# A three-phase audio tower: the last phase's five instruction streams in another order, routing cut in two

## The reference

```
tok:   pad the 750 rows to 3 segments of 256, take every second row -> 3 x 128 tokens;
       per segment softmax(x x^T / 16) x                      -> hidden (32, 384, 256)
attn:  xn = layernorm(hidden); q, k, v = silu(causal conv4(xn Wq / Wk / Wv)); beta = sigmoid(xn Wb)
       delta rule in chunks of 32 per head (T = inv(I + tril(beta k k^T, -1)), state S over chunks)
       branches: short FIR of v, long FIR (63 taps) of v, delta output, v
       gate MLP on [xn, mean and std of each branch] (512 hidden, gelu) -> softmax over 4 branches
       weighted sum of the branches, RMS norm per head, Wo; add hidden
ffn:   y = layernorm(h); z = y proj^T (6 wide); q = tanh(z / 0.3)
       logits = -(6 - q . anchors) / 2 / clip(temp, 0.1); top 2 of 6 experts, softmax over those two
       out = h + sum over experts of weight * (gelu_tanh(y W1[e]) W2[e]),  (384 tokens, 128 hidden)
```

## Time and profile before

| | |
|---|---|
| median of 3 runs | 2969.82 us (2969.29 to 2973.83) |
| profiled execution, its own time | 2961.62 us |
| its span, first to last instruction | 2959.9 us |
| PE busy | 2589.0 us, 87% |
| VectorE, ScalarE, Pool busy | 66%, 46%, 18% |
| granted TensorE clock, mean | 0.872 of full |
| third phase | first matmul at 1031 us, to the end |

### The profile page before, as it was taken

The page is one execution under the profiler, slowest core; times in us unless marked ns, Lnnn a source line. Parts: engine busy times, 40 slices in busy tenths (PEclk is TensorE's granted clock), DMA queues, the critical chain, the costliest instruction groups (busy, mean ns, idle before and its releaser), DMA issues.

```text
span 2959.9 us, 60248 instructions
## 1 busy us (share of the span) xinstructions
PE 2589.0 (87%) x21024; PEld 1966.2 (66%) x21024; DVE 1948.2 (66%) x5272; ACT 1371.9 (46%) x2626; POOL 531.2 (18%) x375
## 2 busy tenths in 40 slices
PE   5888888888699279999999999999999999999997
PEld 3666666666588167677667766776776677767765
DVE  4889888888598125656655665566566656655664
ACT  3777777777222023443444434434434444344342
POOL 1334333334100001111111111111111111111110
PEclk8999999999555557998998999899999999999898
DMA  2666666665566702112111211221131113112200
GB/s 72 206 206 201 200 212 197 212 202 192 198 238 221 207 22 97 63 62 101 61 63 63 101 59 63 68 97 63 57 105 61 63 63 103 61 60 66 97 17 16
DMA packets 233222, 334.12 MB, mean 113 GB/s; under 512 B 113696, under 2 KB 198656, under 8 KB 223776
## 3 DMA queue, kind: packets, MB, share of 16 engines
q1 hardware_dynamic: 207168, 305.89, 31.4%
q10 hardware_dynamic: 24672, 12.58, 1.4%
q0 software_dynamic: 1152, 12.58, 1.1%
HBM read 191.68 MB, written 164.23 MB: 120 GB/s over the span
## 4 chain that ended last, share of the span: by engine, by line
PE 43%; DVE 11%; ACT 5%; issue 5%; DVEq 0%; ACTq 0%
PE bank L1407 6%; PE bank L1417 6%; PE bank L1350 5%; PE bank L1328 3%; PE bank L1361 3%; PE bank L1379 3%; PE bank L1313 3%; PE bank L1245 2%; PE bank L1354 2%; ACT L1554 2%; PE bank L1277 2%; PE bank L1285 2%; DVE HA L1826 1%; DVE bst L1762 1%; PE bank L1370 1%
## 5 line engine op out<-in xcount | busy, mean ns | idle before, releaser
L1417 PE MATMUL bank<-w2e,HE 128*128 128x256 f32 x1152 | 318.6, 417 | 12.5 <-DVE HA L1826 9.6
L1407 PE MATMUL bank<-YT,w1e 128*128 128x384 f32 x768 | 325.9, 552 | 1.3 <-ACT HE L1554 1.3
L683 DVE SCALAR_TENSOR_TENSOR Y<-bank,convw,Y 128x383 f32<-128x383 f32 (+2 forms) x576 | 315.4, 608 | 7.1 <-ACT Y L559 7.1
L1826 DVE SCALAR_TENSOR_TENSOR HA<-bank,we,HA 128x256 f32<-128x256 f32 x576 | 242.7, 477 | 108.0 <-PE bank L1417 105.8
L411 PE MATMUL bank<-pb,wqkv 128*128 128x384 f32 x768 | 288.1, 506 | 10.4 <-DVE pb L667 9.5
L1711 DVE TENSOR_TENSOR L<-bank,b2g 128x48 f32<-128x48 f32 x32 | 6.7, 208 | 412.5 <-PE bank L1361 412.5
L1417 PEld LDWEIGHTS bank<-w2e,HE 128*128 128x128 f32 x1152 | 224.8, 207 | 55.3 <-issue 16.9
L1927 POOL TENSOR_TENSOR ta<-qb,WT 128x768 f32<-128x768 f32 x32 | 72.5, 2266 | 741.5 <-DVE WT L1730 741.5
L1407 PEld LDWEIGHTS bank<-YT,w1e 128*128 128x128 f32 x768 | 153.0, 217 | 77.0 <-issue 30.4
L1350 PE MATMUL bank<-qb,w1g 128*128 128x384 f32 x512 | 201.8, 517 | 0.4 <-ACT GH L1546 0.4
L1537 ACT ACTIVATE ATM<-bank 128x192 f32<-128x192 f32 x192 | 60.2, 331 | 302.2 <-DVE ATM L1653 302.2
(11 more groups left out here) (221 smaller groups left out, 5512.6 us busy)
## 6 DMA issues: line engine op xcount, KB each, us to landing
packa<-pa SPq DMA_DIRECT2D x32, 1932.0 KB, 6.3
qa<-packa SPq DMA_DIRECT2D x32, 1932.0 KB, 7.7
packb<-pb SPq DMA_DIRECT2D x32, 768.0 KB, 5.1
qb<-packb SPq DMA_DIRECT2D x32, 768.0 KB, 6.4
toeplitz<-taps SPq DMA_DIRECT2D x128, 190.0 KB, 4.3
toep<-toeplitz SPq DMA_DIRECT2D x32, 760.0 KB, 4.3
packb<-fsk SPq DMA_DIRECT2D x32, 384.0 KB, 2.3
fl<-fl SPq DMA_DIRECT2D x32, 384.0 KB, 5.0
```

Of the source, the lines that this page charges most:

```text
L683: dve.scalar_tensor_tensor(out=Y[:, j, lag:T], in0=proj_bank[j][:, 0:T - lag], scalar=convw[:, j, CK - 1 - lag:CK - lag], in1=Y[:, j, lag: ...
L1407: mm = pe.matmul(bank[6][:, 0:T], w1e[:, a, k, :], YT[s][:, a, :], start=(a == 0), stop=(a == HALF - 1))
L1417: mm = pe.matmul(expert_bank(b), HE[k % 2][:, b * P:(b + 1) * P], w2e[:, k, :], start=True, stop=True)
L1826: dve.scalar_tensor_tensor(out=HA[s][:, b, :], in0=expert_bank(b), scalar=we[s][:, b, k:k + 1], in1=HA[s][:, b, :], op0=ALU.mult, op1=ALU. ...
```

## The change

- PE: `hidden(f, 3)` before `transpose_mixture`; `gate_s(2)` after `merge_d`; `hidden(e, 0)`, `expert_out(f, 5)` and `route` all between `gate_out` and `updates` 0; `state_update` and `outputs` follow their `updates` with less between them; `expert_out(e, 0)` before `hidden(e, 1)`, `q_state` 2 before `expert_out(e, 1)`. The waits for VB, the diagonal transposes and y's copies stand at other places.
- ScalarE: `gelu_expert(f, 5)` from ahead of the merges' copies to between `gelu_gate` 1 and 2; `gelu_expert(e, 0)` before `copy_update` 0 and the Tanh; the routing's Exp directly behind the Tanh; `copy_update` 2 before `gelu_expert(e, 2)`. `gelu_expert(e, 0)` no longer waits for `expert_out(f, 5)`.
- VectorE: `routing_logits` ends with the logits less their maximum; the ranks are a function of their own behind it. `0.5` goes into `rclip` at setup, and two `tensor_scalar` (L1785, L1787) become one `scalar_tensor_tensor`. `weigh(1)` moves up to stand ahead of `weigh(2)`; `delta_out` before `remainder`; `second_norm` before `add_expert(f, 4)` and `input_stats`; the mixture's sums in another order.
- Pool: 1/sqrt of the second norm first; VB only once y is written (`y_ready`).
- SyncE: the load of the next long FIR follows `weigh(1)` as before, which is now the first mixture step.

The core of the diff (moved code that stays the same inside is cut):

```diff
 PE body
+                    if have_f: hidden(f, s, 3)
                     if have_e: transpose_mixture(e, o)
-                    if have_f: hidden(f, s, 3)
...
                     if have_it:
                         gate_x(it, s, 2)
-                        gate_s(it, 2)
                     if have_n: merge_d(n, o)
                     if have_it:
+                        gate_s(it, 2)
                         gate_x(it, s, 3)
                         gate_s(it, 3)
...
                     if have_it: gate_out(it)
+                    if have_e: hidden(e, o, 0)
+                    if have_f: expert_out(f, 5)
+                    if have_e: route(e, o)
                     if have_n:
                         updates(n, o, 0)
-                    if have_f: expert_out(f, 5)
-                    if have_e: route(e, o)
-                    if have_n:
                         state_update(n, o, 0)
-                    if have_e: hidden(e, o, 0)
-                    if have_n: outputs(n, 0)
+                        outputs(n, 0)
-                    if have_e: hidden(e, o, 1)
+                    if have_e: expert_out(e, 0)
                     if have_n: kb_state(n, o, 1)
-                    if have_e: expert_out(e, 0)
+                    if have_e: hidden(e, o, 1)
                     if have_n:
                         updates(n, o, 1)
                         q_state(n, o, 1)
+                        state_update(n, o, 1)
                         outputs(n, 1)
                     if have_e: hidden(e, o, 2)
                     if have_n:
-                        state_update(n, o, 1)
                         kb_state(n, o, 2)
+                        q_state(n, o, 2)
                     if have_e: expert_out(e, 1)
                     if have_n:
                         updates(n, o, 2)
-                        q_state(n, o, 2)
                         outputs(n, 2)
 ScalarE body, from the last copy of k k^T on (the order after)
+   copy_stats(it); copy_p1(n); copy_u12(n, o); gelu_gate(it, 0); gelu_gate(it, 1)
+   copy_p1b(n); copy_u12b(n, o); gelu_expert(f, 5); gelu_gate(it, 2); gelu_gate(it, 3)
+   copy_y(e, o); gate_exp(it); gelu_expert(e, 0); copy_update(n, 0); route_tanh(e); route_exp(e)
+   gelu_expert(e, 1); copy_update(n, 1); squares(it, s); copy_update(n, 2); gelu_expert(e, 2)
 VectorE
-                    dve.tensor_scalar(beats, lg, -float(ND), 0.5, ALU.add, ALU.mult)
-                    dve.tensor_scalar(lg, beats, rclip[:, 0:1], None, ALU.mult)
+                    dve.scalar_tensor_tensor(out=lg, in0=lg, scalar=-float(ND), in1=rclip.broadcast, op0=ALU.add, op1=ALU.mult)
+                    dve.tensor_reduce(me, lg, AX.X, ALU.max); dve.tensor_tensor(rank, lg, me, ALU.subtract)  # lr_ready
 VectorE body, from gate_logits on (the order after)
+   gate_logits(it); add_expert(f, s, 5); gate_weights(it); weigh(it, s, 1); weigh(it, s, 2); state(n, 0)
+   routing_logits(e); routing_ranks(e); delta_out(n, o, 0); remainder(n, 1); routing_weights(e, o)
+   mix_add 2; add_expert(e, o, 0); delta_out(n, o, 1); mix_add 3; state(n, 1); mix_add 4; remainder(n, 2)
 Pool
+                    if e is not None: wait veps_ready; br = bv ** -0.5
                     if n is not None:
+                        if e is not None: pool.wait_ge(*y_ready.now(e))
                         VB = v * beta
-                    if e is not None: wait veps_ready; br = bv ** -0.5
```

More of the change, by code:

```diff
@@ L1476, in body @@
                         gate_out(it)
-                    if have_n:
-                        if have_e:
-                            pe.wait_ge(*yT0_copied.now(e))
-                        updates(n, o, 0)
+                    if have_e:
+                        hidden(e, o, 0)
                     if have_f:
@@ L1485, in body @@
                     if have_n:
+                        if have_e:
+                            pe.wait_ge(*yT0_copied.now(e))
+                        updates(n, o, 0)
                         state_update(n, o, 0)
+                        outputs(n, 0)
                     if have_e:
-                        hidden(e, o, 0)
+                        expert_out(e, 0)
                     if have_n:
-                        outputs(n, 0)
+                        kb_state(n, o, 1)
                     if have_e:
@@ L1549, in gelu_expert, with copy_mixture @@
                     act.wait_ge(*hid_ready.now(e, k + 1))
[L1550 to L1553, removed]
+                    act.wait_ge(*eo_ready.now(e, k - 1))
                     act.activation(HE[k % 2][:, :], bank[6][:, 0:T], ACT.Gelu_apprx_tanh).then_inc(he_ready.sem, 1)
+                def copy_mixture(e):
+                    act.wait_ge(*onT_ready.now(e, 1))
+                    copy(ONT[:, 0, :], bank[5][:, 0:T]).then_inc(onT0_copied.sem, 1)
+                    act.wait_ge(*onT_ready.now(e, 2))
+                    copy(ONT[:, 1, :], bank[4][:, 0:T]).then_inc(onT1_copied.sem, 1)
@@ new lines, in copy_u12, with copy_p1b @@
+                def copy_u12(n, s):
+                    act.wait_ge(*u12_ready.now(n))
+                    copy(UF[s][0:SC, :, SC:2 * SC], blocks(0, slice(0, SC), SC))
+                    copy(TL[SC:2 * SC, :, 0:SC], blocks(0, slice(SC, 2 * SC), SC))
+                    copy(UF[s][2 * SC:3 * SC, :, 3 * SC:P], blocks(1, slice(2 * SC, 3 * SC), SC)).then_inc(u12_copied.sem, 1)
+                def copy_p1b(n):
+                    act.wait_ge(*p1b_ready.now(n))
+                    copy(P1B[DH:P, 0:6, :], blocks(0, slice(DH, P), DH))
+                    copy(P1B[DH:P, 6:NM, :], blocks(1, slice(DH, P), DH)).then_inc(p1b_copied.sem, 1)
@@ new lines, in copy_u12b, with copy_y @@
+                def copy_u12b(n, s):
+                    act.wait_ge(*u12b_ready.now(n))
+                    copy(UF[s][0:DH, 0:6, DH:P], blocks(0, slice(0, DH), DH))
+                    copy(UF[s][0:DH, 6:NM, DH:P], blocks(1, slice(0, DH), DH)).then_inc(u12b_copied.sem, 1)
+                def copy_y(e, s):
+                    act.wait_ge(*yT_ready.now(e, 1))
+                    copy(YT[s][:, 0, :], bank[2][:, 0:T]).then_inc(yT0_copied.sem, 1)
+                    act.wait_ge(*yT_ready.now(e, 2))
+                    copy(YT[s][:, 1, :], bank[6][:, 0:T]).then_inc(yT1_copied.sem, 1)
@@ L1564, in body @@
                     if have_e:
[L1565 to L1570, removed]
+                        copy_mixture(e)
                     if have_n:
```

157 lines of the change are left out of this document (83 added, 74 removed).

## The result

| | us | ratio to the kernel before (95% interval) |
|---|---|---|
| kernel before, same chip | 2969.56 median (2968.85 to 2973.83) | |
| changed kernel | 3044.27 median (3041.98 to 3061.39) | 1.0261 [1.0229, 1.0294] |
| forecast | 3064 (2965 to 3140) | slower, with a chance of 0.81 |

The change costs 75 us; the profiled span grew from 2959.9 to 3040.2. The direction was right and the size 20 us too large.

A forecast was written before the change was run, and what follows sets the result against it. PE, busy 87% of the span, was taken to set the pace. +2.85 us a pass over 30 passes (+85) and +9 for the clock gave 3056 profiled, 3064 as median, range 2965 to 3140.

The forecast's parts named there:

- P1 copied earlier: ScalarE ahead of `merge_b`: gelu and table load leave, so PE's wait there goes, -0.45 us a pass.
- The gelu of expert 5: ScalarE between gate gelus: one table load each way makes PE wait at `gate_out`, +1.56 us a pass, bounds 0 and 1.6.
- The drain of 1.38 us per switch: ScalarE table switches: the skill's extra charge would make the `gate_out` wait 4.3 us; the sum left it out.
- Order behind `gate_out`: From `gate_out` to `updates` 1: VectorE and Pool taking turns delay `remainder`, +1.8 us a pass, bounds 0 and 2.3.
- its lock: VectorE two-input or two-port instructions and reading Pool ones exclude each other: with it +1.8 us before `updates` 1, without it 0.
- VB behind y: Pool's VB no longer beside L1750, which falls to about 0.95 us; the wait at `transpose_mixture` goes, -0.06 a pass.
- The rest: Waits for the state and W, masks, moved SyncE load: 0 a pass, bounds -0.3 and +0.3.
- The clock: PE's granted clock: more drops, partly hidden by waits, +0.3 us a pass, bounds -4.65 and +4.2.
- The rival in which the clock takes it all back: PE stays at 2.4 GHz behind `gate_out`, wins 4.65 a pass against 2.85: 2916 us, chance 0.12.
- the sum, 2.85 + 0.3: Per pass: waits -0.45 + 1.56 + 1.8 - 0.06 = +2.85 us, plus +0.3 for the clock.
- the marks named ahead: Signs in the new profile of table loads, waits, step ends and clock that would show the forecast right or wrong.

The follow-up runs named there:

- e1: Changed kernel with the gelu of expert 5 on ScalarE moved back ahead of the P1 copies: 2974.5 us.
- e9: Kernel before with the gelu of expert 5 behind the u12b copies, ahead of gate gelu 2, and `gate_s(2)` behind `merge_d`: 3039.3 us.
- e6: Kernel before with the gelu of expert 5 between gate gelus 1 and 2, ahead of the u12b copies, `gate_s(2)` left in place: 2951.5 us.
- e3: Changed kernel with Pool's two branch products held until the mixture's first sum is done, v product first: 3068.5 us.
- e2: Changed kernel with PE's wait for the diagonal transposes one step earlier, ahead of `products` 2: 3003.4 us.
- e10: Changed kernel with gelu 5 back ahead of the P1 copies, the diagonal-transposes wait ahead of `products` 2, `weigh(1)` behind `remainder(1)`: 2926.4 us.
- e7: Kernel before with the Sqrt of the variances on ScalarE moved from behind kk copies 2 and 3 to ahead of the gelu of expert 4: 2942.3 us.
- e12: e10 with Pool's v product first and its FIR product behind mixture step 3: 2913.6 us.
- e4: Changed kernel with `weigh(1)` back behind `remainder(1)` on VectorE and the long FIR load behind mixture step 2 again: 3024.7 us.

## Why the prediction was right in its direction, point by point

- *P1 copied earlier, -0.45:* shown. The wait at `merge_b` is gone in the changed kernel and comes back in e1 (10.9 in 24).
- *The gelu of expert 5, +1.56:* the wait is there with 1.45, and the chain behind `merge_d` measured 5.12 of 5.1. One load each way was right. What the step left out is the clock: alone on the kernel before, the same edit cost +0.77 idle and +1.91 by the clock (e9), 69 us where 33 were worked out. I held that it decides itself by table loads; e6 shows that it is decided by what stands ahead of them (the copies of u12b, `gate_s(2)`).
- *The page of the Trainium skill ("ScalarE: Activation LUTs", Table sets: the hidden batching unit)* told against the edit, and rightly for its place. The drain of 1.38 us per switch (same page, What ACT_TABLE_LOAD costs) is not in the trace, where in the chain shown above each gelu follows its load by 0.01 to 0.02 us. e6 goes against the rule as I used it: a load more at the gate gelus, and 19 us less.
- *Order behind `gate_out`, +1.8:* at the full clock this is right, and as a mean over the passes it was mis-sized. The chain is as described: weighs, ta and tb in turn, the product ending with tb, first weigh to `updates` 1 +1.55 (7.94 against 6.39), and in e1's passes at the full clock `updates` 1 comes 15.52 us behind `gate_out` (+1.95). But as idle time it came to +0.40 at `updates` 1 and +0.45 at `state_update`, 0.85. The sum used 1.43 us as the wait before and 2.7 after; the means are 0.96 and 1.37. In 8 of the 23 waits it is 2.26; in the other 15 more of the stretch is at 1.2 GHz, PE arrives later and waits 0.7 to 1.0. I had named that cover under the clock, but priced cover and clock together at +0.3.
- *The page of the Trainium skill ("SBUF — State Buffer", Who interferes with whom):* its lock fits the durations read here, the weigh of 2.25 and the product of 0.94 us (0.95 and 0.27 with Pool idle, e3).
- *VB behind y:* shown, L1781 at 0.958 us and no wait for it.
- *The rest, 0:* here the prediction missed +0.46 at `transpose_stats` and +0.55 of work. The wait for tdiag was moved to stand there, behind that for the kk copy, with those for the deviations, the means and the bank: five. The kk copy is the last to come: it ends at 1676.83, PE's queue has the wait for it at 1676.87, waits that stand behind it at 1676.96 and 1677.07, the weight load at 1677.14, and PE starts at 1677.17. I had named the moved wait in the text of the change and given it no price; e2 shows 0.29 of the 0.46 to be that one. Of the work, part stands at the waits: `updates` 0 takes 1.08 us, of which 0.16 lay under the next step before (0.92 between the starts); with the wait for W behind it the whole 1.08 counts. The rest is not explained; e1 takes half of the work away.
- *The clock, +0.3:* net +0.14, in the 0.89 to 0.94 named. The rival in which the clock takes it all back was wrong for this kernel, which stayed at 0.93; e10, with three of the edits taken back, runs at 0.96 and below the kernel before.

So the sum, 2.85 + 0.3 against 2.94, is closer than its terms, and that is luck: 0.95 too much for the order, 1.0 missed elsewhere. Of the marks named ahead, all held: two loads at the gate gelus, 1.5 us at `gate_out`, nothing at `merge_b`, over 2 us at `updates` 1 where the clock is full at the wait (8 of 23), tb and the product ending together, more than 14 us from `gate_out` to `updates` 1 (17.2, part of it at 1.2 GHz).

## What to carry to other kernels

Price a moved activation from the event that its engine waits for, not only by its table loads: put loads into that engine's idle time, ahead of a wait that it has anyway, and they cost nothing here (e6); behind it they stand on the path. Count the waits in front of an instruction, and let those that are long fulfilled be taken by an earlier one. Where the granted clock sits between its levels, every wait of a microsecond can have a second price in the clock, more than twice the first (e9), small (e7) or of the other sign (e12); only a run tells, so test each edit alone, and take a reordering apart before throwing it away: here one edit of many cost 69 us and hid a gain.

## What the runs showed of the hardware that was not expected

- The same kernel work gets from 4.4 to 12.7 us a pass at 1.2 GHz by the order of the instructions alone. The idle time does not say which: e2 has 6.03 idle and 5.87 at the lower level, e9 has 4.50 and 12.70. The falls come at few places, counted from the start of `gate_out`: 0.4 to 5 us behind it in all kernels; 9 to 13 us in the changed kernel and e2, in the steps behind `updates` 0; 14.6 to 17.2 in the kernel before, just behind the start of `updates` 1; and at the loop's turn.
- The wait ahead of `gate_out` goes with a fall behind it. In the five kernels where PE waits 1.4 to 1.5 us there (changed, e2, e3, e4, e9) all 25 passes have a fall within 5 us behind the start of `gate_out`; in the other nine it is 7 to 18 of 25 (12 before, 18 in e1). How long the clock then stays down differs (3.7 us a pass in e2, 9.0 in e9), and why is open.
- Putting matmuls nobody needs into a wait made the changed kernel 27 us faster (e5).
- A product of 128x108 on VectorE takes 0.27 us with Pool idle (e3) and 0.94 beside Pool's 128x768 product; one of 128x18 with a scalar takes 0.18 and 1.05.
